# Four image attention layers in one kernel: the last layer weighs two key tiles in one run of column-tiled matmuls, with a three-slot ring of weights

## The reference, cut to what matters

```python
x = _group_norm(hidden_states, gn_gamma, gn_beta)
x = x.reshape(B, C, H * W).transpose(0, 2, 1)
q, k, v = x @ wq.T + bq, x @ wk.T + bk, x @ wv.T + bv      # 8 heads of 32
scores = jnp.einsum('bhid,bhjd->bhij', q * scale, k)
probs = jax.nn.softmax(scores, axis=-1)
ctx = jnp.einsum('bhij,bhjd->bhid', probs, v)
out = _layer_norm(ctx @ wo.T + bo, ln_gamma, ln_beta)
return out + residual            # residual: the output of layer 2
```

## Time and profile before

| | |
|---|---|
| time, median of 3 runs | 2812.36 us (2811.44 to 2816.11) |
| span of the profiled execution | 2818.8 us |
| TensorE busy | 2605.2 us, 92% |
| VectorE, ScalarE, GpSimdE busy | 66%, 46%, 21% |
| TensorE's mean granted clock | 0.928 |
| mean DMA traffic | 26 GB/s |
| one "both", from image to image | 332 to 334 us |

### The profile page before, as it was taken

The page is one execution under the profiler, slowest core; times in us unless marked ns, Lnnn a source line. Parts: engine busy times, 40 slices in busy tenths (PEclk is TensorE's granted clock), DMA queues, the critical chain, the costliest instruction groups (busy, mean ns, idle before and its releaser), DMA issues.

```text
span 2818.8 us, 26455 instructions
## 1 busy us (share of the span) xinstructions
PE 2605.2 (92%) x9892; PEld 1429.7 (51%) x9892; DVE 1864.0 (66%) x1925; ACT 1291.2 (46%) x2209; POOL 597.3 (21%) x322
## 2 busy tenths in 40 slices
PE   7979988989999999999999999998999999978887
PEld 4556653464644646454564645546464455643332
DVE  4544227687477765777666875868656876568985
ACT  3353221646345462555526454364624546135466
POOL 0083120050110501023020401105010040224473
PEclk8999996989999899999999899998999899989898
DMA  2000010010202002020110202010020200222200
GB/s 88 1 0 1 1 30 16 9 37 1 75 1 45 1 8 68 1 45 1 49 27 1 45 1 75 1 30 16 1 75 1 45 1 16 45 45 46 46 1 30
DMA packets 29297, 72.15 MB, mean 26 GB/s; under 512 B 10224, under 2 KB 10416, under 8 KB 28912
## 3 DMA queue, kind: packets, MB, share of 16 engines
q1 hardware_dynamic: 29168, 70.45, 10.0%
HBM read 11.40 MB, written 8.39 MB: 7 GB/s over the span
## 4 chain that ended last, share of the span: by engine, by line
PE 70%; DVE 17%; ACT 4%; SPq 4%; issue 3%; POOL 2%; DMA 1%; DVEq 0%; ACTq 0%; POOLq 0%
PE ps L632 11%; PE ps L665 11%; PE ps L651 9%; PE ps L783 8%; PE ps L952 7%; PE ps L874 6%; PE ps L640 4%; PE ps L787 4%; DVE ba_nmx L1328 4%; SPq L496 3%; DVE fa_nmx L1328 2%; PE ps L721 2%; PE ps L860 2%; DVE accb L1496 2%; DVE xm L1381 1%
## 5 line engine op out<-in xcount | busy, mean ns | idle before, releaser
L1181 ACT ACTIVATE prb<-ps 128x512 f32<-128x512 f32 x896 | 493.5, 603 | 318.2 <-PE ps L665 294.6
L1328 DVE TENSOR_REDUCE ba_nmx<-ps 128x1 f32<-128x1024 f32 x448 | 529.0, 1218 | 129.4 <-PE ps L651 129.3
L1496 DVE TENSOR_TENSOR accb<-accb,prb 128x1024 f32<-128x1024 f32 x312 | 385.4, 1263 | 90.2 <-ACT prb L1181 89.0
L665 PE MATMUL ps<-qs,ks 97*128 97x512 f32 x896 | 366.1, 484 | 37.2 <-DMA qs<-ba_nmx_r 28.1
L1042 ACT ACTIVATE pr<-ps 128x512 f32<-128x512 f32 x336 | 195.9, 596 | 360.0 <-PE ps L874 271.9
L651 PE MATMUL ps<-ks,qs 96*128 96x512 f32 x896 | 330.2, 475 | 26.5 <-DVE ba_nmx L1328 15.9
L554 POOL TENSOR_TENSOR q2k<-pr,q2k 128x512 fp32r<-128x512 f32 x112 | 145.8, 1318 | 845.6 <-ACT q2k L1079 845.6
L665 PEld LDWEIGHTS ps<-qs,ks 97*128 97x128 f32 x896 | 165.9, 203 | 286.0 <-ACT prb L1181 179.5
L952 PE MATMUL ps<-prb,vb 128*32 128x512 f32 x1792 | 249.5, 630 | 2.6 <-ACT prb L1181 2.5
L651 PEld LDWEIGHTS ps<-ks,qs 96*128 96x128 f32 x896 | 174.9, 210 | 145.9 <-DVE ba_nmx L1328 75.0
L1328 DVE TENSOR_REDUCE fa_nmx<-ps 128x1 f32<-128x1024 f32 x168 | 198.1, 1216 | 47.6 <-PE ps L860 37.1
(11 more groups left out here) (320 smaller groups left out, 3562.3 us busy)
## 6 DMA issues: line engine op xcount, KB each, us to landing
qs<-part SPq DMA_DIRECT2D x168, 128.0 KB, 2.4
ks<-part SPq DMA_DIRECT2D x168, 128.0 KB, 2.4
xm<-in_x SPq DMA_DIRECT2D x8, 1024.0 KB, 5.7
out<-prb SPq DMA_DIRECT2D x28, 256.0 KB, 2.7
q2k<-part SPq DMA_DIRECT2D x48, 128.0 KB, 2.4
w<-in_weights SPq DMA_DIRECT2D x1, 2592.0 KB, 8.8
out<-pr SPq DMA_DIRECT2D x4, 256.0 KB, 2.0
qs<-ba_nmx_r SPq DMA_DIRECT2D x56, 4.0 KB, 1.8
```

Source lines behind the costliest of these rows:

```text
L665: return pe.matmul(o.ps[:, bank, :], keys[0:ROW + 1, tile(jt)], queries[0:ROW + 1, cols(ic)], start=True, stop=True)
L1181: act.activation(weights3(o, s, g), o.ps[:, turn3[score_use(s, g) % 3], :], ACT.Exp)\
L1328: dve.tensor_reduce(o.nmx[:, head, it:it + 1], o.ps[:, bank:bank + 2, :], AX.XY, ALU.max, negate=True).then_inc(o.max_sb[n].sem, 1)
L1496: dve.tensor_tensor(o.sums[pair], o.pairs[(s - 1) % 2][pair] if j == 1 else o.sums[pair], o.pairs[s % 2][pair], ALU.add).then_inc(done.sem, 1)
```

## The change

`RUN = 2`: `weigh` takes two steps at once, sixteen instructions in a row, after the first two scores of every second step. `RING = 3`: the weights have three slots, step n of the image uses slot n mod 3, and the exponentials of step n wait for the weighing that covers step n-3 and for the sum of step n-3. The memory of the third slot is that of the third `xm` buffer; images alternate between two. So `xm` of image b must be free early. After layer 2 SyncE writes it to device memory (`kept`, 1 MB), and as soon as that write has landed and the group norm of the last layer has read `xm`, image b+2 is loaded into the same buffer. At the end of back(b) the residual comes back in two DMAs of 512 KB into the third slot (`again`); VectorE waits for them before the end of the layer norm. All tables of `ORDER` are new.

```diff
+RUN = 2
+RING = 3
-        xm = [sb(f"xm{n}", [P, CH, T]) for n in range(3)]
+        xm = [sb(f"xm{n}", [P, CH, T]) for n in range(2)]
+        kept = nc.dram_tensor("kept", (B, C, T), F32, kind="Internal").ap().rearrange("b (h p) t -> b p h t", p=P)
-        prb = sb("prb", [P, 2, QUAD, IW])
+        prb = sb("prb", [P, RING, QUAD, IW])
...
                 def back(b):
+                    sp.wait_ge(front_of(b).res[2].sem, front_of(b).res[2].at(b, 4))
+                    sp.dma_start(kept[b], xm[b % 2][:]).then_inc(o.kept.sem, 16)
+                    yield
+                    if b + 2 < B:
+                        sp.wait_ge(o.gn[3]["h"].sem, o.gn[3]["h"].at(b, CH))
+                        sp.wait_ge(o.kept.sem, o.kept.at(b, 16))
+                        sp.dma_start(xm[b % 2][:], x_v[b + 2]).then_inc(x_loaded[b % 2].sem, 16)
+                    yield
                     for u in range(CH):
                         yield from stacks(b, u)
                         yield from shift_rows(b, u)
                         if u == 0:
                             yield "head"
+
+                    sp.wait_ge(o.kept.sem, o.kept.at(b, 16))
+                    sp.wait_ge(o.weighed[3].sem, o.weighed[3].at(b, CH * STEPS3 // RUN - 1))
+                    for pair in range(2):
+                        sp.wait_ge(o.summed3[pair].sem, o.summed3[pair].at(b, (NT - 1) * IC * CH - 2))
+                    for ch in range(CH):
+                        sp.dma_start(residual(o, ch), kept[b, :, ch, :].rearrange("p (i n) -> p i n", i=IC)).then_inc(o.again.sem, 16)
+                    yield
                     for ic in range(IC):
-                        if ic and b + 3 < B:
-                            sp.wait_ge(o.l3_g.sem, o.l3_g.at(b, 4))
-                            sp.dma_start(xm[b % 3][:], x_v[b + 3]).then_inc(x_loaded[b % 3].sem, 16)
...
-                        def weigh(s):
-
-                            ic, jt = divmod(s, NT)
-                            n = STEPS3 * u + s
-                            pe.wait_ge(o.exped[3].sem, o.exped[3].at(b, QUAD * (n + 1)))
-                            if jt == 0 and n:
+                        def weigh(first):
+
+                            n = STEPS3 * u + first
+                            pe.wait_ge(o.exped[3].sem, o.exped[3].at(b, QUAD * (n + RUN)))
+                            if first % NT == 0 and n:
                                 pe.wait_ge(o.taken[3].sem, o.taken[3].at(b, n // NT))
+                            for s in range(first, first + RUN):
+                                jt = s % NT
+                                for g in range(QUAD):
...
-                            if s:
-                                weigh(s - 1)
+                            if s and s % RUN == 0:
+                                weigh(s - RUN)
                                 yield
...
-                            if n >= 2 and g == 2 * pair:
-
-                                act.wait_ge(o.weighed[3].sem, o.weighed[3].at(b, n - 1))
-
-                                chunk, j = divmod(n - 2, NT)
+                            if n >= RING and g == 2 * pair:
+
+                                act.wait_ge(o.weighed[3].sem, o.weighed[3].at(b, (n - RING) // RUN + 1))
+
+                                chunk, j = divmod(n - RING, NT)
...
+                    dve.wait_ge(o.again.sem, o.again.at(b, 16 * CH))
                     for ic in range(IC):
...
-                                                     scalar=vcol("ln_w", ch), in1=xm[b % 3][:, ch, cols(ic)],
+                                                     scalar=vcol("ln_w", ch), in1=residual(o, ch)[:, ic, :],
```

One line of the old tables, of 55, and what stands first in its place (the numbers are lengths of runs, alternately from the one generator and the other):

```diff
     ("backs", "PE"): (
-        5, 1, 2, 3, 2, 4, 2, 2, 1, 3, 1, 2, 1, 1, 1, 2, 1, 6, 2, 13, 1, 3, 1, 5, 1, 1, 1, 4, 2, 2, 1, 3, 1, 1,
+        0, 1, 2, 1, 3, 2, 4, 5, 1, 1, 1, 2, 1, 3, 1, 3, 1, 4, 1, 1, 1, 3, 1, 3, 1, 3, 2, 5, 1, 2, 1, 1, 1, 5,
```

More of the change, by code:

```diff
@@ L355, in back_lane @@
             o.scored, o.exped = alone("scored", CH * STEPS3 * QUAD), alone("exped", CH * STEPS3 * QUAD)
[L356 removed]
+            o.weighed = alone("weighed", CH * STEPS3 // RUN)
             o.summed3 = [alone(f"summed{pair}", (NT - 1) * IC * CH)[3] for pair in range(2)]
@@ L367, in back_lane @@
             o.stored = alone("stored", 16 * 4)[3]
+            o.kept, o.again = alone("kept", 16)[3], alone("again", 16 * CH)[3]
             group_norm_of(o, in_turn, 3)
@@ L378, in attention_layers @@
         setup_products = signal("setup_products")
-        x_loaded = [Signal(semaphore(f"x_loaded{n}"), list(range(n, B, 3)), 16) for n in range(3)]
+        x_loaded = [Signal(semaphore(f"x_loaded{n}"), list(range(n, B, 2)), 16) for n in range(2)]
         fronts = (
@@ L468, in _ @@
             sp.dma_start(cst[:], constants).then_inc(loaded.sem, 16)
-            for b in range(3):
+            for b in range(2):
                 sp.dma_start(xm[b][:], x_v[b]).then_inc(x_loaded[b].sem, 16)
@@ L1194, in back @@
                     if b == B - 1:
-                        act.wait_ge(backs[0].l3_g.sem, backs[0].l3_g.at(B - 3, 4))
+                        act.wait_ge(backs[0].gn[3]["h"].sem, backs[0].gn[3]["h"].at(B - 2, CH))
+                        act.wait_ge(backs[0].kept.sem, backs[0].kept.at(B - 2, 16))
                     take_values(b, 3, 0, o.vb, 0)
@@ L1508, in back @@
                     if b == B - 1:
-                        dve.wait_ge(backs[0].l3_g.sem, backs[0].l3_g.at(B - 3, 4))
+                        dve.wait_ge(backs[0].gn[3]["h"].sem, backs[0].gn[3]["h"].at(B - 2, CH))
+                        dve.wait_ge(backs[0].kept.sem, backs[0].kept.at(B - 2, 16))
                     take_values(b, 3, 1, o.vb, 2)
```

93 lines of the change are left out of this document (48 added, 45 removed), and 43 rows, old and new, of the table ORDER.

## The result

| | before | changed kernel |
|---|---|---|
| time, median | 2814.08 us (2811.44 to 2816.11, 4 runs) | 2794.24 us (2787.21 to 2798.57, 4 runs) |
| ratio, 95% interval | | 0.9926 [0.9907, 0.9945] |
| span of the profiled execution | 2818.8 us | 2796.8 us |
| TensorE's mean granted clock | 0.928 | 0.934 |
| one "both" | 333, 333, 331, 334, 332 us | 327, 327, 328, 333, 329 us |

Faster by 20 us, where 28 were forecast. The changed kernel was timed again with the experiments: 2792.56 us, from 2782.8 to 2798.3. Its six runs there lie 15.5 us apart; those of the kernel before lie 5, 6, 10 and 13 us apart in its four series of 4, 11, 11 and 29 runs.

The account below looks back on a forecast made before the run. TensorE's stream was taken to bound "both", with VectorE nearly full in parts of "backs". The terms -24.4 + 3 - 0.6 - 6 gave -28 us, from 2812.4 to 2784 us, range 2765 to 2806.

Parts of the forecast that it names:

- Fewer visits: TensorE in "both": 26 instead of 40 visits to column-tiled mode, 0.29 us each, saving 24.4 us over six.
- The border inside a run: Between a run's two weighings on TensorE: no extra time, as the next weights load under running matmuls; 0 us.
- Rival 1: Border inside a run costs 0.10 us, or runs end waiting for ScalarE, and "backs" gives nothing: 2800 us; chance 0.17.
- The longer run costs nothing while ScalarE has room: In "both", TensorE's run of about 1.9 us stalls ScalarE at most a few tenths, covered by its room: 0 us.
- Other moves of the tables: In "both", reordered tables keep their pieces and count: 0 us, bound 2 us each way per "both".
- Trip and load of x: SyncE between two backs: residual write and image load make the stacks late, +0.5 us per "both", 3 us in all.
- Rival 4: SyncE's queue between two backs: transfers get in front of the stacks, 2812 or 2846 us; chance 0.08.
- "backs", -6: Last images regrouped: maxima with sixteen steps, then sixteen of image 7 alone, 131 us instead of 137; gain 6 us.
- Rival 2: In "backs" the maxima section does not shrink, losing 14 us instead of gaining 6: 2804 us; chance 0.09.
- Rival 3: The 0.29 us belong to each weighing on TensorE, so a run of two pays twice: 2809 us; chance 0.06.
- What it said would show it: Signs in the later profile, among them a "both" of 328 to 330 us instead of 332 to 334.

Follow-up runs that it names:

- split_runs: Changed kernel with the two weighings of a run parted again by one score matmul, 14 of 16 runs per image: 2835.80 us.
- no_round_trip: Changed kernel without writing the residual to `kept` and reading it back, so the last layer's residual is left out: 2791.14 us.
- x_load_behind_stacks: Changed kernel with the load of the next image's x issued behind the first round's stacks instead of ahead of them: 2790.99 us.
- vector_adds_alone: Changed kernel with VectorE making all additions in the last image's second round and GpSimdE none: 2781.45 us.
- keys_first: Changed kernel with two of the back's projections ahead of those of `xm` in TensorE's table of "both": 2809.09 us.

## Why the prediction was right, and which steps failed

The side, the range (2765 to 2806) and a gain of tens of us were right. The point was 10 us too low. That it came so near is in part luck, as the steps show:

*Fewer visits, -24.4.* The count holds, 40 and 26 in a "both". The price holds under the new tables: 0.29 forecast, 0.28 and 0.33 measured by split_runs. It is not a price that every order pays: under the old tables it is 0.09. From before to the changed kernel the work fell by 13.5 us in five "both" where 20.3 were forecast, 0.19 a visit. The order has its part in it either way: with single weighings the new tables have 6.0 us more work than the old ones (1507.8 against 1501.8), with runs of two 6.0 less (1489.6 against 1495.6).

*The border inside a run, 0.* Right: the added passes take 0.43 us each, even less than 0.45. The rule of TensorE: Matmul & The Clock Gate of the Trainium skill ("Part 3", "The mechanism"), by which weight loads with equal row groups wait for the array, is not what the trace shows here. Rival 1's border isn't there.

*The longer run costs nothing while ScalarE has room.* The condition that it named, waits for exponentials behind each run if the cover is gone, is what happened under the old tables: 44 waits instead of 15. ScalarE's room over a whole "both" (162 of 334 us busy) was not the cover: it is as large under the old tables, 160 us a "both". The cover is what the table puts between two runs.

*Other moves of the tables, 0 with 2 us each way per "both".* **This is the step that failed.** With runs of two the tables are worth 2848.6 - 2792.6 = 56 us, and five "both" differ by 44.3, 8.9 us each, where the bound was 2. The prediction took runs and tables for terms that add; the square shows +36, +23 and together -20. It looked at the order's pieces and their count, and costed nothing for where the waits fall.

*The clock, not in the sum at all.* TensorE is busy for 44 us less at the lower level in five "both" of the repeat, which is 22 us of the gain; in the first profile it is 33 and 16. That is as much as the forecast's largest term or nearly so. The prediction read the clock in its views (0.94 in a "both") and had no step for it. That the missing terms, +12 idle and -16 to -22 clock, are of opposite sign, and that the work fell short by 7, made five "both" come out near the forecast's -17.8: -18.9 and -23.5. That is luck.

*Trip and load of x, +3.* Mis-sized: 0. It had the write land beside the group norm's end and the load run into the stacks. The write lands 3 us ahead of the load's issue and of the end of the group norm, and the load takes 4.9 us instead of 5.7. Rival 4 fell with it; no_round_trip and x_load_behind_stacks confirm.

*"backs", -6.* Not seen. From image 7's first maxima to the end it is +5.3 in the first profile and +2.1 in the repeat. The 32 visits were saved there too: TensorE's work fell from 236.5 to 227.7 us, 8.8 for the 9.3 forecast. But its idle time grew from 46.4 to 51.7, and the cost of the lower clock from 29.5 to 38.3 (34.9 in the repeat). In the two sections that the step added up, 129 + 2 = 131 us were forecast for 137. The maxima section took 74.9 us for the forecast 67, at a mean clock of 0.80 where the section that served as its model had 0.92. Image 7 alone took 69.5 and 66.5, where the forecast had 62: 4.2 to 4.3 us a step. The step that gave way was the 4.1 us a step with 4 more for two without additions; ScalarE, GpSimdE and VectorE are all between 37 and 46 of 69.5 us busy, none full, and TensorE 59.7. vector_adds_alone shows that some 6 us of it go with the additions of the two engines side by side, in part by way of the clock.

*Rivals.* Rival 2 (the last image, 2804) had the place right and too large a loss: 14 us for the measured 7 in the two sections (4 in the repeat). Rival 3 is refuted by split_runs.

*What it said would show it.* "both" of 328 to 330 us: measured 327 to 333. The 333 is one "both" with 37.5 us at the lower clock, where the same one of the repeat has 23.9 and takes 327.6. Half of those 13.6 us more lie at the end of the 2.7 us wait for `tmp` and in the eight projections of `xm` behind it. The row is the first profile; in the repeat the same eight are issued at clock 1.00:

```profile
1784.20:1791.00 6.80, 6.17 (x8) 2.57 (x9) 1.90 (x3) 0.00 (x0) 0.00 (x0) 0.50 0.02 2
```
```profile
1782.20:1785.80 3.60, 3.52 (x8) 1.63 (x9) 1.35 (x3) 0.00 (x0) 0.00 (x0) 1.00 0.03 3
```

So such dips fall in one execution and not in the next. They are the likely reason for the 15 us between runs: of the six runs of the repeat the fastest has a mean granted clock of 0.938, the two slowest 0.932 and 0.934. That link was not tested further.

## What to carry to other kernels

Where engines follow an order written out by hand, a longer instruction block and the order around it are one change: build the square (old order and new, each with and without the block) before giving either a price. On a kernel bound by TensorE, write the time at the lower clock of each stretch beside its idle time. Waits of 2.15 and 0.94 us behind small transposes were followed by the lower clock in every image and cost 17 us over the program. One wait of 2.7 us among full projections was followed by full clock in most images of the changed kernel, but not in all. And where GpSimdE and VectorE add side by side in a tail, try VectorE alone: that gave 11 us here, and with it a version that beats both kernels (2781 and 2780 us).

## What the runs showed of the hardware

A small VectorE operation is held by a GpSimdE addition that starts just before it. VectorE and GpSimdE in the changed kernel, in the group norm between two backs:

```profile
1704.51 0.16 DVE L1429 TENSOR_TENSOR ba_gn_dev_sq<-ba_gn_dev 128x2 f32<-128x2 f32 x1
1704.71 2.33 DVE L1432 TENSOR_TENSOR ba_gn_var<-ba_gn_dev_sq,ba_gn_mv 128x2 f32<-128x2 f32 x1
```
```profile
1704.68 2.34 POOL L562 TENSOR_TENSOR acc<-pr 128x1024 f32<-128x1024 f32 x1 [96.21 <-ACT pr L1061]
```

Two elements per partition take 2.33 us, until the GpSimdE operation is over. The two meet so in all six "both" of the changed kernel. In the kernel before they never meet, and the same operation takes 0.16 us for every image. So this collision came with the new tables; it is behind the wait for `ba_gn_var` above, 1.2 us in each "both". SBUF — State Buffer of the Trainium skill, under "SBUF: two separate sides", states such a lock: an operation of VectorE with two inputs in SBUF and one of GpSimdE that reads SBUF shut each other out, and who starts first keeps the ports to its end. The trace agrees, 2.33 us beside 2.34.

In a run of two weighings the passes that come on top are slightly quicker than the first: 0.43 us each for the two added, against 0.45.

Whether the granted clock falls behind TensorE's 32-row transposes depends on the order around them. In the kernel before and in keys_first a stretch at the lower level starts within 9 us of them in each of six images, 3.4 to 10.2 us long; with the changed kernel's table there is none within 14 us. At the place shown above, 3.44 of 4 us busy was followed by full clock and 1.30 of 4 by 10 us at half. Elsewhere the same instructions were followed by either level in different executions, as behind the wait for `tmp`.
